# Attention of a graph network on one Trainium2 core: POOL's gathers wait, two at a time, for PE's sum of a tile

## The chip, the cores and the metric

The kernel runs on one core of one Trainium2 chip. The metric is the time on the device in microseconds (us) for one execution; lower is better. Engines are called PE (matmul), PEld (its weight load), DVE (vector), ACT (scalar), POOL (GpSimd) and SP (which issues DMAs).

## The reference

There are 6250 nodes of 128 features and 206250 edges, sorted by their target node `dst`. Two layers follow one another, each on `relu(layernorm(x))` and each with a residual. The change lies in the first:

```
h = (x @ W.T).reshape(N, 4, 32)
alpha = leaky_relu((h*att_src).sum(-1)[src] + (h*att_dst).sum(-1)[dst])
w = exp(alpha - segment_max(alpha, dst)[dst]);  w = w / segment_sum(w, dst)[dst]
out = segment_sum(h[src] * w[:, :, None], dst)
```

The second layer is an MLP on `[x[dst], x[src], edge_attr]` for each edge, summed over `src`'s partner in the same way; the change doesn't touch it.

## The kernel before, in words

The edges are cut into 1612 tiles of 128 edges, and the tiles into `NB` = 62 batches of `BT` = 26. The attention runs over the batches; a batch is a row of 26 turns, one for each tile, on PE, ACT and DVE, which are tied together by semaphores only. Each engine's order is written out by hand; the loops (`Fori`) hold two batches, `q` = 0 and 1.

In turn t of batch b:

- **DVE** makes the one-hot rows of tile t of batch b+2 (`hot`, L934), adds PE's sum of tile t-2 of batch b to the accumulator (`add_up`, L1041), and does one step of the softmax chain of batch b+1 (`chain`; at turn 4 the step "logits", which waits for all 26 gathers of batch b+1) or some products of messages (`product`, L1021, which ends in `msg_ready`).
- **PE** transposes the one-hot rows (`turn`, L1452), expands the node terms of tile t-1 of batch b+2 (`expand`, L1462), and sums the messages of tile t of batch b by a matmul with the one-hot rows (L1524), which raises `agg_ready`.
- **ACT** copies PE's transposed rows out (`turn_out`, L620) and widens one-hot rows to f32 (`widen`, L627).
- **POOL** does nothing in the attention but gather. `gather(i, q)` fetches for each tile of batch b = 2i+q the rows `h[src]` by one indirect DMA of 128 rows of 528 bytes into `G[:, q, t, :]` (L491). There are two slots `q`, so the gathers of batch b overwrite those of batch b-2 and run while batch b-2 is summed. They wait for the products of b-2 that read them: the first 13 for message pieces 0 and 1, the other 13 for pieces 2 and 3. So they come in two bursts of 13.

The order of PE within a turn matters below: `turn(b+2, t)`, then `expand(b+2, t-1)`, which waits for ACT's copy of tile t-1, and then the sum of tile t. ACT in turn waits for PE's transposes, and DVE's `add_up` for PE's sum; PE has two PSUM banks for each of the two.

At the end of the attention (L507) POOL waits for all sums, and does vector work for the nodes. In the target stretch of the second layer POOL scatters a finished tile by an indirect DMA (L541), in groups of three or four that wait for ACT's copies of them (L702). In the source stretch it issues one gather with addition at a time (L555), each behind a wait.

Of the kernel before, what the change touches and what calls it, by code (L numbers as in the profile page):

```python
# [25 lines left out]
BT = 26  # L26
# [39 lines left out]
def gnn(nc, x, src, dst, ea, W, asrc, adst, bias, W1, b1, W2, b2, out):  # L66
# [12 lines left out]
    with ctx:  # L79
# [4 lines left out]
        def sem(name):  # L84
            if name not in sems:
                sems[name] = ctx.enter_context(nc.semaphore(name))
            return sems[name]
# [355 lines left out]
        def _(pool):  # L443
# [39 lines left out]
            def gather(i, q, first=False):  # L483
                pool.wait_ge(sem("idx_ready"), 2 * i + q + 1)
                for h in range(2):

                    if not first:
                        pool.wait_ge(sem("msg_ready"), 4 * (2 * i + q - 2) + 2 * h + 2)
                    pool.nop(nofuse=True)
                    for t in range(h * (BT // 2), (h + 1) * (BT // 2)):  # L490
                        pool.indirect_dma_start(G[:, q, t, :], None, h_tab,  # L491
                                                bass.IndirectOffsetOnAxis(ap=idx[:, q, t:t + 1], axis=0)
                                                ).then_inc(sem(f"gath{q}"), 16)
            gather(0, 0, True)
            pool.wait_ge(sem("cols_used"), 2)
            gather(0, 1, True)
            pool.wait_ge(sem("hx_used"), NCH)
            M.memset(zlate, 0.0).then_inc(sem("zl_ready"), 1)
# [5 lines left out]
            with pool.Fori(1, NB // 2) as i:  # L504
                for q in range(2):
                    gather(i, q)
# [1241 lines left out]
```

## Time and profile before

| | us |
|---|---|
| median of 3 runs | 8049.95 |
| the runs | 8098.06, 8049.95, 8049.9 |
| the profiled execution, its own time | 8039.81 |
| its span, first to last instruction | 8038.0 |
| mean granted clock of TensorE in it | 0.808 |

The stages in the profiled span: preparation to about 200 us, attention to about 3770 us, node work to about 3900 us, targets to about 6650 us, sources to the end. "Slices" below are 40 equal parts of the span, so one is 201 us.

### The profile page before, as it was taken

To read this page: it belongs to the slowest core of one execution; us is meant where nothing else is said; L and a number is where in the kernel's file an instruction comes from. 1 tells how busy PE (TensorE), PEld (TensorE's weight loads), DVE (VectorE), ACT (ScalarE), POOL (GpSimd) and SP (SyncE) were. 2 spreads that over 40 slices of the span, in tenths; PEclk is the share of its full clock that TensorE was granted. 3 is DMA by queue.
4 is the path that set the end of the run, shared out by engine and by line. 5 is a ranking of instruction groups with operands and counts; after the bars stand their busy time and mean duration, and the time that the engine had idled before them with its cause. 6 is when DMAs were issued, how large, how long until landed. Compare 5 with 4: busy or idle time off the path is not lost.

```text
span 8038.0 us, 156599 instructions
## 1 busy us (share of the span) xinstructions
PE 5687.3 (71%) x34498; PEld 4372.6 (54%) x34499; DVE 4041.5 (50%) x14406; ACT 2887.4 (36%) x8241; POOL 3876.0 (48%) x3713
## 2 busy tenths in 40 slices
PE   4555555555555555555777878877877778999999
PEld 3444444444444444444555555555555556777777
DVE  5444444444444444446433434333333337888887
ACT  2333333333333333333222222222222226777776
POOL 4444344443444444443555555555555555555553
PEclk6666666667666666667889898898988889999999
DMA  3311111111111111113766666666656667999998
GB/s 86 110 31 30 29 31 31 30 31 29 31 31 30 30 30 31 31 31 111 210 188 194 194 196 196 197 191 189 192 168 202 188 190 189 213 213 213 215 212 197
DMA packets 860288, 993.30 MB, mean 124 GB/s; under 512 B 307992, under 2 KB 663224, under 8 KB 859774
## 3 DMA queue, kind: packets, MB, share of 16 engines
q1 hardware_dynamic: 662494, 608.23, 28.4%
q0 software_dynamic: 190592, 378.22, 17.6%
q10 hardware_dynamic: 6816, 3.38, 0.1%
q14 instruction: 348, 2.85, 0.1%
q8 instruction: 38, 0.62, 0.0%
HBM read 726.65 MB, written 262.76 MB: 123 GB/s over the span
## 4 chain that ended last, share of the span: by engine, by line
PE 55%; another core or an unknown queue 18%; issue 14%; DVE 8%; DVEq 3%; ACT 2%; DMA 1%; ACTq 0%; SPq 0%; POOLq 0%
PE bank L1524 12%; PE bank L1683 9%; PE bank L1618 8%; PE bank L1616 7%; PE bank L1673 5%; PE bank L1452 3%; PE bank L1462 2%; PE bank L1606 2%; DVEq L246 1%; DVE arena L1041 1%; PE bank L1571 1%; PE bank L1664 1%; DVE arena L1190 1%; ACT arena L620 1%
## 5 line engine op out<-in xcount | busy, mean ns | idle before, releaser
L491 POOL DMA_INDIRECT arena<-h_tab,arena x1612 | 1550.1, 962 | 2119.4 <-DVE arena L1021 1620.4
L541 POOL DMA_INDIRECT xr<-arena x1612 | 1581.5, 981 | 1233.9 <-ACT arena L702 753.9
L1524 PE MATMUL bank<-arena 128*128 128x136 f32 x6448 | 1527.6, 374 | 92.5 <-DVE arena L1041 9.5
L1041 DVE TENSOR_TENSOR arena<-arena,bank 128x272 f32 x1612 | 695.5, 431 | 1669.0 <-remote 1175.7
L620 ACT ACTIVATE arena<-bank 128x256 bf16<-128x256 bf16 x1612 | 617.5, 383 | 2413.1 <-remote 1190.1
L1618 PE MATMUL bank<-arena 128*128 128x256 f32 x3224 | 1107.3, 428 | 472.5 <-DVE arena L1251 383.6
L702 ACT ACTIVATE arena<-bank 128x256 f32<-128x256 f32 x1612 | 601.1, 384 | 2138.0 <-PE bank L1618 1276.8
L1462 PE MATMUL bank<-arena 128*128 x3224 | 427.8, 188 | 1273.5 <-ACT arena L620 641.4
L1524 PEld LDWEIGHTS bank<-arena 128*128 128x128 f32 x6448 | 1150.6, 247 | 178.3 <-issue 111.0
L1616 PE MATMUL bank<-arena 128*128 128x256 f32 x3224 | 1104.9, 427 | 11.6 <-DVE arena L1235 9.7
L1462 PEld LDWEIGHTS bank<-arena 128*128 128x128 bf16 x3224 | 325.3, 113 | 1378.3 <-issue 1343.1
L1618 PEld LDWEIGHTS bank<-arena 128*128 128x128 f32 x3224 | 650.2, 211 | 692.7 <-DVE arena L1251 482.4
L555 POOL DMA_INDIRECT arena<-p_tab,arena x428 | 667.8, 1560 | 662.0 <-DMA arena<-p_tab,arena 434.7
L1683 PE MATMUL bank<-arena 128*128 128x257 f32 x3424 | 897.4, 384 | 4.3 <-ACT arena L779 2.9
L1251 DVE COPY arena<-bank 128x128 f32<-128x128 f32 x806 | 233.2, 289 | 900.6 <-PE bank L1606 357.9
L627 ACT ACTIVATE arena<-arena 128x256 f32<-128x256 bf16 x1612 | 645.7, 408 | 87.1 <-issue 66.6
L1235 DVE TENSOR_SCALAR arena<-arena 128x128 f32<-128x128 bf16 x1612 | 471.6, 300 | 386.1 <-PE bank L1618 239.3
L1616 PEld LDWEIGHTS bank<-arena 128*128 128x128 f32 x3224 | 595.2, 217 | 113.4 <-issue 45.0
L1452 PE MATMUL bank<-arena 128*128 128x128 bf16 x3224 | 542.6, 260 | 123.4 <-DVE arena L934 112.5
L1683 PEld LDWEIGHTS bank<-arena 128*128 128x128 f32 x3424 | 584.9, 191 | 75.6 <-issue 6.5
L779 ACT ACTIVATE arena<-arena 128x512 f32<-128x512 f32 x856 | 535.5, 626 | 98.4 <-DVE arena L1346 77.9
L1673 PE MATMUL bank<-arena 128*128 x3852 | 566.7, 274 | 2.3 <-DVE arena L1346 1.7
(253 smaller groups left out, 6954.6 us busy)
## 6 DMA issues: line engine op xcount, KB each, us to landing
arena<-xr SPq DMA_DIRECT2D x428, 516.0 KB
arena<-q_tab SPq DMA_DIRECT2D x1612, 128.0 KB
arena<-in_edge_attr SPq DMA_DIRECT2D x61, 832.0 KB
arena<-rel_tab SPq DMA_DIRECT2D x124, 224.0 KB
arena<-h_tab,arena POOLq DMA_INDIRECT x1612
xr<-arena POOLq DMA_INDIRECT x1612
arena<-rel_tab SPq DMA_DIRECT2D x124, 192.0 KB
xr<-arena SPq DMA_DIRECT2D x26, 516.0 KB
```

What stands on the lines that cost most here:

```text
L491: pool.indirect_dma_start(G[:, q, t, :], None, h_tab, bass.IndirectOffsetOnAxis(ap=idx[:, q, t:t + 1], axis=0)).then_inc(sem(f"gath{q}"), 16)
L541: pool.indirect_dma_start(xr, bass.IndirectOffsetOnAxis(ap=pos[:, q, t:t + 1], axis=0), Rb[:, t, :], None).then_inc(sem(f"scat{m}"), 16)
L555: pool.indirect_dma_start(XR[:, s, k, RW:RW + HID], None, p_tab, bass.IndirectOffsetOnAxis(ap=sidx[:, s, k:k + 1], axis=0), compute_op=ALU ...
L620: A.activation(ohT[:, t % 2, :], PSB[t % 2][:].bitcast(BF16)[:, 0:2 * P], ACT.Copy).then_inc(sem("ohT_ready"), 1)
L1041: V.tensor_tensor(a, a, PSB[3 + t % 2][:, 0:2 * H * MW], ALU.add).then_inc(sem("acc_done"), 1)
L1452: last = pe.transpose(PSB[t % 2][:].bitcast(BF16)[:, k * P:(k + 1) * P], OHb[:, s, t, k * P:(k + 1) * P], identb)
L1462: last = pe.matmul(ab_ps[half][:, j, :, :].rearrange("p s c -> p (s c)"), ohT[:, t % 2, k * P:(k + 1) * P], flat(aT3[:, bass.ds(regs[t] + ...
L1524: last = pe.matmul(PSB[3 + t % 2][:, k * H * MW:(k + 1) * H * MW], OH[:, (t + 2 * q) % 4, k * P:(k + 1) * P], flat(msg[:, t, :, :]), start ...
L1616: pe.matmul(o, OHT[:, (t + 2 * q) % 4, :], Qw[:, t, :], start=True, stop=False)
L1618: pe.matmul(o, EAT[:, (t // 2 + q) % 2, :], w1z[:, t % 2, :], start=False, stop=True).then_inc(sem("main_done"), 1)
L1673: last = pe.matmul(PSB[2 + m % 2][:, j * HID:(j + 1) * HID], ohTp[:, m % 2, j, :], flat(Pt[:, bass.ds(reg, 1), part, :]), start=(part == 0 ...
L1683: last = pe.matmul(PSB[4 + m % 2][:, 0:XW], OHp[:, m, j, :], hid[:, m % 2, j, :], start=(j == 0), stop=(j == PR - 1))
```

## The change

Within each half, the gather of every odd tile first waits until PE has summed the tile of the same number in the batch whose slot it overwrites. The gather of the next (even) tile follows it at once. The first two batches, which overwrite nothing, are as before.

```
@@ gather(i, q, first=False)
                     pool.nop(nofuse=True)
                     for t in range(h * (BT // 2), (h + 1) * (BT // 2)):
+                        if not first and t % 2 == 1:
+                            pool.wait_ge(sem("agg_ready"), BT * (2 * i + q - 2) + t + 1)
+                            pool.nop(nofuse=True)
                         pool.indirect_dma_start(G[:, q, t, :], None, h_tab,
                                                 bass.IndirectOffsetOnAxis(ap=idx[:, q, t:t + 1], axis=0)
                                                 ).then_inc(sem(f"gath{q}"), 16)
```

## Rows read from the trace of the kernel before

**Rows 1.** The page: the granted clock in 40 slices, in tenths.
```profile
PEclk6666666667666666667889898898988889999999
```

**Rows 2.** Windows of attention, targets and sources: busy us (instructions) by engine.
```profile
400.00:3600.00 3200.00, 1793.45 (x12608) 1526.97 (x12608) 1487.92 (x5593) 1027.55 (x3203) 1338.02 (x1404) 0.68 0.13 30
4300.00:5900.00 1600.00, 1269.74 (x6293) 857.49 (x6291) 626.88 (x2243) 382.71 (x1104) 907.74 (x926) 0.90 0.66 193
6800.00:7800.00 1000.00, 984.33 (x6467) 776.98 (x6464) 813.08 (x2908) 738.13 (x1941) 504.00 (x323) 1.00 0.91 213
```

**Rows 3.** The timeline of POOL over two bursts of 13 gathers.
```profile
2008.45 0.95 POOL L491 DMA_INDIRECT arena<-h_tab,arena  x1 [15.56 <-DVE arena L1021]
2009.71 0.95 POOL L491 DMA_INDIRECT arena<-h_tab,arena  x1 [0.31 <-issue]
...
2023.53 0.95 POOL L491 DMA_INDIRECT arena<-h_tab,arena  x1 [0.30 <-issue]
2034.86 0.95 POOL L491 DMA_INDIRECT arena<-h_tab,arena  x1 [10.38 <-DVE arena L1021]
...
2049.98 0.95 POOL L491 DMA_INDIRECT arena<-h_tab,arena  x1 [0.30 <-issue]
```

**Rows 4.** Windows of one batch, DVE's L1041 alone (one per turn): us, busy (x).
```profile
2008.45:2026.80 18.35, 1.75 (x4) 0.55 0.21 49
2026.80:2034.86 8.06, 2.68 (x7) 0.75 0.00 0
2034.86:2053.20 18.34, 2.07 (x5) 0.67 0.22 48
2053.20:2065.48 12.28, 4.73 (x11) 0.80 0.00 1
```

**Rows 5.** The timeline of ACT inside the second of these bursts.
```profile
2042.75 0.38 ACT L620 ACTIVATE arena<-bank 128x256 bf16<-128x256 bf16 x1 [4.35 <-issue]
...
2051.32 0.39 ACT L620 ACTIVATE arena<-bank 128x256 bf16<-128x256 bf16 x1 [7.88 <-issue]
```

**Rows 6.** The timeline of PE at the same place.
```profile
2044.81 0.42 PE L1452 MATMUL bank<-arena 128*128 128x128 bf16 x2
2051.86 0.35 PE L1462 MATMUL bank<-arena 128*128 x2 [6.63 <-issue]
```

**Rows 7.** Windows: data movement after the first burst: us, busy of five engines, clock, DMA share.
```profile
2010.00:2024.50 14.50, 7.05 (x35) 5.90 (x35) 4.56 (x17) 2.80 (x10) 11.13 (x12) 0.51 0.25 57
2024.50:2026.20 1.70, 0.00 (x0) 0.00 (x0) 0.54 (x3) 0.28 (x1) 0.00 (x0) 0.50 0.19 40
2026.20:2027.40 1.20, 0.82 (x4) 0.70 (x5) 0.45 (x2) 1.20 (x5) 0.00 (x0) 0.50 0.00 0
```

**Rows 8.** The waits of 400 to 3600 us: engine and line, for whom, us, times, longest.
```profile
POOL arena L491 <- DVE arena L1021: 1457.5, 108, 16.5
...
DVE arena L1041 <- remote: 1076.8, 218, 10.6
ACT arena L620 <- remote: 1018.4, 142, 10.6
```

**Rows 9.** Line L491, 400 to 3600 us: shortest, median and longest duration in ns.
```profile
L491 POOL DMA_INDIRECT arena<-h_tab,arena x1404: 946/952/1002, 411.2 to 3585.6; - x176
```

**Rows 10.** Windows of the last two batches, L1524 alone (four matmuls per turn).
```profile
3720.00:3770.80 50.80, 37.70 (x208) 30.59 (x208) 0.90 0.11 33
```

**Rows 11.** The timeline of DVE from the last sum of batch 60 on.
```profile
3747.80 0.44 DVE L1041 TENSOR_TENSOR arena<-arena,bank 128x272 f32 x1 [0.34 <-PE bank L1524]
...
3750.66 0.44 DVE L1041 TENSOR_TENSOR arena<-arena,bank 128x272 f32 x1
...
3752.65 0.44 DVE L1041 TENSOR_TENSOR arena<-arena,bank 128x272 f32 x1 [0.38 <-PE bank L1524]
```

**Rows 12.** The waits of ACT and PE in the targets, 4300 to 5900 us.
```profile
ACT arena L702 <- issue: 278.8, 198, 4.7
...
ACT arena L702 <- remote: 237.2, 83, 8.2
...
PE bank L1618 <- DVE arena L1251: 218.1, 107, 6.5
PE bank L1618 <- issue: 49.6, 35, 6.0
```

**Rows 13.** Sources: ACT's longest group of waits (6800 to 7800 us), and one gather.
```profile
ACT arena L763 <- PE bank L1664: 125.0, 216, 1.2
...
7002.04 1.58 POOL L555 DMA_INDIRECT arena<-p_tab,arena  x1 [1.82 <-DMA arena<-p_tab,arena]
```

More of the change, by code:

```diff
@@ L490, in gather @@
                     for t in range(h * (BT // 2), (h + 1) * (BT // 2)):
+                        if not first and t % 2 == 1:
+                            pool.wait_ge(sem("agg_ready"), BT * (2 * i + q - 2) + t + 1)
+                            pool.nop(nofuse=True)
                         pool.indirect_dma_start(G[:, q, t, :], None, h_tab,
```

## The prediction, made before the changed kernel was run

> **What bounds the kernel now.** I began with the page's slices: the attention, about 45% of the span, has a granted clock of 0.6 to 0.7 where the last stages have 0.9 [rows 1]. In the windows by stage no engine is the bound there: in 3200 us PE is busy 1793, DVE 1488, ACT 1028 and POOL 1338 [rows 2]. 1404 gathers in these 3200 us are 54 batches, so a batch takes 3200 / 54 = 59.3 us. An engine with 33 us of work in 59 doesn't set that; something stops all of them.
>
> The timeline of POOL shows where to look. Its 26 gathers of a batch come in two bursts of 13, each gather 1.256 us behind the last (2009.71 - 2008.45), so a burst lasts 13 x 1.256 = 16.3 us, and POOL then waits 10 to 16 us for the next pieces of messages [rows 3, 8]. I cut one batch into four windows at these borders, the burst with the 2 us or so until its last data are in, and counted DVE's sums, one for each turn [rows 4]. Outside the bursts 7 + 11 = 18 turns take 8.06 + 12.28 = 20.3 us, 1.13 us each. Inside them 4 + 5 = 9 turns take 36.7 us, 4.1 us each. That is the finding on which all else rests: while gathers are issued back to back, the other engines hardly get on.
>
> How they stand still: PE ends the transposes of a tile at 2045.23 (2044.81 + 0.42) and ACT's copy of such rows starts at 2051.32, after 7.88 us of idleness that the profile puts down to nothing; PE then waits 6.63 us for that copy [rows 5, 6]. DVE has 218 such waits on "remote", 1077 us in all, and ACT 142, 1018 us; none of them has a late producer that the profile shows [rows 8]. The standstill ends with the burst: the last gather of the burst starts at 2049.98, ACT goes on 1.3 us later.
>
> **The price of a gather now.** In the four windows, bursts cost 36.7 us, less 9 turns at 1.13 (10.2 us), less about 3 us for the border between two batches (register loads and the factor), which falls into the first burst; I size it by the last batches, where the sum of the last tile and of the next batch's first are 3750.66 - 3747.80 = 2.9 us apart [rows 4, 11]. That leaves 23.5 us, or 0.90 us for each of 26 gathers; I use 0.93, the mean of this and of the same count with the border at 1.5 us (0.96). A batch with gathers that cost nothing would take 59.3 - 26 x 0.93 = 35.1 us. Two rows bear this out: the last two batches gather nothing and take 50.8 / 2 = 25.4 us, without the work on tiles of the batch two ahead [rows 10]; and 26 turns at 1.13 with the border are 29.4 + 3 = 32.4 us.
>
> **The change part by part.**
>
> *Added waits.* 13 for each of 60 batches (2 to 61), each a register sum, a wait and a nop on POOL's queue. Behind such a wait stand only the rest of the gathers; POOL has no other work in the attention, and its work for the nodes waits for all sums anyway. POOL needs 26 x 1.256 = 32.7 us for a batch's gathers. The waits have no row of their own; between gathers stand 0.30 us today [rows 3]. The cost on POOL lies between 0 (inside these 0.30) and 13 x 0.3 = 3.9 us, so its floor is 32.7 to 36.6 us per batch, below or near the 35.1 of the others. I count nothing on the path, as the forecast batch is far above both.
>
> *Moved gathers.* Now gather 1 goes when tile 1 of batch b-2 is summed, then 2 and 3, and so on; the last, tile 25, goes when PE has summed tile 25 of b-2. Who waits for that is DVE's step "logits" at turn 4 of batch b-1, behind `add_up` of tile 2. In the last batches tile 25's sum and tile 2's of the next batch are 3752.65 - 3747.80 = 4.85 us apart at DVE [rows 11]. One gather needs some 0.95 us of issue, and the traffic of a burst is over at most 2.7 us after its last gather began (2026.20 - 2023.53; no traffic after) [rows 3, 7]. So 2.7 of 4.85 us, hidden, with room for one or two gathers of arrears. POOL collects arrears when turns are faster than 1.256 us, as they are outside bursts (1.13): 26 turns x 0.13 = 3.3 us at most, from which the slow border of batches subtracts 3. Counted at nothing; with the cover gone (arrears of three gathers, 3.8 us) DVE waits 2.7 + 3.8 - 4.85 = 1.7 us per batch, 100 us in all.
>
> *What the spacing removes.* This is the term that decides. With the two-gather steps, a pair takes 2.5 us and two turns take at least 2.3, so POOL pauses only as long as the engines are held up; but that is also when it counts: as soon as DVE, ACT and PE stand still, POOL stops within two gathers instead of running on for up to 13. The trace of before has no pairs in the attention, so the price per gather after has bounds. Upper: 0.93, today's. Lower: 0, from the sources, where single gathers come 3.1 us apart (1000 / 323), traffic is at 0.91, and the longest wait in ACT's largest group is 1.2 us; nothing is held up [rows 2, 13]. Below nothing is excluded: no gather can speed the engines over having none. Between them lie the targets: 926 scatters in groups of 3 and 4 that sometimes run together. If all of PE's waits at L1618 were theirs, that is (218.1 + 49.6) / 926 = 0.29 us each; if I take ACT's waits without a producer, (278.8 + 237.2) / 926 = 0.56 us each, again the most [rows 2, 12]. These are nearest to what the change makes: short groups, at times joined. I take the middle, 0.43 us. The attention has tighter buffers (two banks, not four), which speaks for more; pairs are shorter than those groups, which speaks for less.
>
> *The sum.* A batch then takes 35.1 + 26 x 0.43 = 46.3 us, 13.0 less than 59.3. Over 60 batches that is 780 us: 8040 - 780 = 7260 for the profiled execution, whose 8039.8 lies 10 us below the median of the runs; against the median, 7270. In general the time is 8050 - 1560 x (0.93 - p) for a price p. A denser attention should also raise the granted clock there above 0.68, as the windows outside bursts (0.75 and 0.80) show against 0.55 in the first burst [rows 2, 4]; this is contained in the pace of 1.13 and not counted again.
>
> *A rule against it.* All of L491's gathers take 946 to 1002 ns, so DVE doesn't hold up POOL's descriptors at all [rows 9], and data movement is at a quarter of its capacity in a burst [rows 7]. The Trainium skill (SBUF — State Buffer, in the consequences drawn from the port table) states "DMA never contends with a compute engine", and knows only the reverse, a DVE instruction that starves POOL's descriptor generation. By that rule the bursts would hold nothing up, p would stay at 0.93 and the time at 8050; by the rows the engines stand still in just these windows. The trace has the decision, and I can't name the mechanism from it.
>
> **The rivals.**
>
> *1. The burst isn't the cause (nothing gained, 8050).* The bursts start on DVE's products, so they always lie at the same turns (about 0 to 3 and 11 to 15); the standstill could belong to these turns, to the chain's steps or the loading of instructions. For it: the fixed place. Against it: waits without a producer are there in the targets too, beside scatters, and not in the sources with their spaced gathers [rows 12, 13]. The rule above gives the same time. 0.09.
>
> *2. A fixed price per gather or per group (slower).* If each group of gathers costs a fixed standstill of some microseconds, 13 pairs replace two bursts. The point of decision is 24.2 / 13 = 1.9 us per pair. ACT's shortest standstills in the second burst are over 4 us [rows 5]; a pair costs at most what it and its landing last, 2.5 + 1.5 = 4 us, but of this about half is covered by buffers. At 2.1 us per pair a batch takes 35.1 + 27.3 + 1.7 for late gathers = 64.1 us, 4.8 more: 8050 + 60 x 4.8 = 8340. 0.10.
>
> *3. Pairs cost nothing, POOL becomes the bound.* Then a batch takes POOL's floor of 36 to 38 us: at 37, 60 x 22.3 = 1340 us less, 6710. For it: the sources. Against: POOL would then issue without a pause, which is the burst again. 0.12, with prices below 0.25 (up to 6990).
>
> *4. The pairs join.* When turns run at 1.13 us POOL has no pause, gathers join to groups of 6 to 10, and the price is 0.70 to 0.88: 7690 to 7970. 0.11.
>
> **How the numbers follow.** The forecast (price 0.25 to 0.70, 6990 to 7690) has 0.58; its likeliest is 7270. The range should leave out no more than 2 in 10: it goes from 6900 (part of rival 3) to 7950 (nearly all of rival 4), and leaves out rivals 1 and 2 and the lower end of 3. A measurement of this kernel can tell about 1% from no change. Faster by over 1%: 0.58 + 0.12 + 0.11 = 0.81; within 1%: rival 1, 0.09; slower: rival 2, 0.10.
>
> **What would show it.** After the change POOL's L491 should stand in pairs with pauses of a microsecond or so, released by PE at L1524, and its waits on DVE at L1021 should be gone. A batch should last 46 us, the attention end near 2990 instead of 3770 us, and later stages be unchanged. DVE's waits on "remote" at L1041 should fall from 1077 to some 450 us, and the longest from 10.6 to about 4 us. The clock in the attention should be above 0.70. Rival 3 shows as POOL without idleness; rival 4 as long rows of gathers behind idleness of 0.30 us; rival 1 as standstills at turns 3 and 14 beside a pausing POOL; rival 2 as 13 of them in a batch. A wait of DVE at L953 for a gather would show late gathers. What would make me wrong most likely is the price of a pair, which no row of this kernel measures in a loop as tight as the attention's.

## The result

| | before | after |
|---|---|---|
| median, us | 8054.2 (4 runs, 8049.9 to 8098.1) | 7419.5 (4 runs, 7395.8 to 7434.7) |
| ratio, 95% interval | | 0.920 (0.916 to 0.923) |
| span of the profiled execution | 8038.0 | 7415.3 |
| mean granted clock | 0.808 | 0.828 |

The change saves 635 us. The forecast was 7270 in a range of 6900 to 7950. The experiments below are compared apart from this table, each with the kernel before on its own chip.

The changed kernel's lines are three further down from L494 on (L491 is L494, L1524 is L1527, L1041 is L1044). The page's clock in 40 slices of what is now a shorter span, as in [rows 1]:

```profile
PEclk6777777766767776779988888898888889999999
```

Windows of three stretches, to be laid beside [rows 2] (busy us and instructions of PE, PEld, DVE, ACT, POOL; clock; DMA share; GB/s):

```profile
400.00:2900.00 2500.00, 1807.33 (x11880) 1530.26 (x11881) 1424.75 (x5273) 959.68 (x3019) 1305.21 (x1332) 0.71 0.17 37
3700.00:5300.00 1600.00, 1277.29 (x6281) 863.10 (x6281) 625.39 (x2231) 379.26 (x1098) 904.86 (x921) 0.89 0.66 192
6200.00:7200.00 1000.00, 984.58 (x6471) 777.75 (x6469) 814.14 (x2910) 738.94 (x1941) 505.46 (x324) 1.00 0.92 213
```

1332 gathers in 2500 us are 51.2 batches, 48.8 us each instead of 59.3; 10.5 us less in 60 batches are 630 us, the whole gain. Targets and sources move as much per us as before (921 scatters in 1600 us beside 926, 324 gathers in 1000 beside 323). So nothing was given back later.

POOL's timeline over some gathers, to be read beside [rows 3]:

```profile
2032.58 0.95 POOL L494 DMA_INDIRECT arena<-h_tab,arena  x1 [6.92 <-PE bank L1527]
2033.84 0.95 POOL L494 DMA_INDIRECT arena<-h_tab,arena  x1 [0.30 <-issue]
2035.38 0.95 POOL L494 DMA_INDIRECT arena<-h_tab,arena  x1 [0.60 <-issue]
...
2039.34 0.99 POOL L494 DMA_INDIRECT arena<-h_tab,arena  x1 [1.75 <-PE bank L1527]
...
2049.28 0.95 POOL L494 DMA_INDIRECT arena<-h_tab,arena  x1 [4.19 <-issue]
2050.53 0.95 POOL L494 DMA_INDIRECT arena<-h_tab,arena  x1 [0.30 <-issue]
2051.79 0.95 POOL L494 DMA_INDIRECT arena<-h_tab,arena  x1 [0.30 <-issue]
2053.05 0.95 POOL L494 DMA_INDIRECT arena<-h_tab,arena  x1 [0.30 <-issue]
2054.31 0.95 POOL L494 DMA_INDIRECT arena<-h_tab,arena  x1 [0.30 <-issue]
2055.57 0.95 POOL L494 DMA_INDIRECT arena<-h_tab,arena  x1 [0.30 <-issue]
```

The wait is PE's now, as meant. But the gathers often don't come in pairs: six stand together at 2049.28. POOL had fallen behind (ahead of them it stood idle for 4.19 us that no late producer explains), all its waits were fulfilled, and it ran on until it caught up. Counted over 600 to 2000 us, with a gap of 0.5 us or more as the border of a group, 745 gathers stand in 280 groups: 195 pairs, 75 fours, 9 sixes and one alone, 2.7 on average. The other engines pay for the joined ones, as ACT's timeline shows:

```profile
2057.18 0.38 ACT L623 ACTIVATE arena<-bank 128x256 bf16<-128x256 bf16 x1 [5.86 <-remote]
```

The waits of 400 to 2900 us, beside [rows 8]:

```profile
ACT arena L623 <- PE bank L1455: 915.9, 755, 4.6
POOL arena L494 <- PE bank L1527: 728.4, 367, 7.0
DVE arena L1044 <- PE bank L1527: 591.4, 596, 3.9
...
ACT arena L623 <- remote: 412.2, 148, 5.9
...
DVE arena L1044 <- remote: 214.4, 97, 5.2
```

DVE's waits on "remote" fall from 1077 us in 54 batches to 214 in 51, ACT's from 1018 to 412, and the longest from over 10 to under 6 us. This reads better than it is, for part of the late waits only has another label now: the rows that name PE as the releaser were these before.

```profile
ACT arena L620 <- PE bank L1452: 707.8, 812, 4.0
DVE arena L1041 <- PE bank L1524: 327.9, 442, 4.7
```

Both labels together, DVE waited for PE's sums (1076.8 + 327.9) / 54 = 26.0 us per batch and now waits (214.4 + 591.4) / 51.2 = 15.7. These 10.3 us are nearly the 10.5 by which a batch got shorter. No group of DVE's waits names a gather: none came late.

### The profile page after: what moved, and what is told of

It reads as the page before. It is cut to its first block, busy times and chain, and to the rows that moved or that the text cites. A ratio compares the mean times of both kernels' runs of the same rounds, so it can differ in the third digit from the quotient of the medians.

```text
span 7415.3 us, 158159 instructions
## 1 busy us (share of the span) xinstructions
PE 5830.3 (79%) x34498; PEld 4483.9 (60%) x34499; DVE 4072.9 (55%) x14406; ACT 2876.8 (39%) x8241; POOL 3921.0 (53%) x3713
## 4 chain that ended last, share of the span: by engine, by line
PE 66%; another core or an unknown queue 12%; issue 10%; DVE 6%; DVEq 3%; ACT 2%; DMA 1%; ACTq 0%; POOL 0%; SPq 0%; POOLq 0%
PE bank L1527 16%; PE bank L1686 10%; PE bank L1621 9%; PE bank L1619 8%; PE bank L1676 6%; PE bank L1455 4%; PE bank L1465 4%; PE bank L1609 2%; DVEq L246 2%; ACT arena L623 1%; PE bank L1574 1%; PE bank L1667 1%; DVE arena L1193 1%; DVE arena L1238 1%
## 5 line engine op out<-in xcount | busy, mean ns | idle before, releaser
L494 POOL DMA_INDIRECT arena<-h_tab,arena x1612 | 1592.0, 988 | 1474.2 <-PE bank L1527 857.6
L1527 PE MATMUL bank<-arena 128*128 128x136 f32 x6448 | 1625.0, 392 | 77.6 <-DVE arena L1044 6.2
L1527 PEld LDWEIGHTS bank<-arena 128*128 128x128 f32 x6448 | 1227.4, 263 | 149.2 <-issue 108.6
L1044 DVE TENSOR_TENSOR arena<-arena,bank 128x272 f32 x1612 | 699.9, 434 | 1006.3 <-PE bank L1527 689.8
L1621 PEld LDWEIGHTS bank<-arena 128*128 128x128 f32 x3224 | 655.6, 212 | 707.7 <-DVE arena L1254 450.2
L1465 PE MATMUL bank<-arena 128*128 x3224 | 442.3, 193 | 526.5 <-ACT arena L623 406.5
L1465 PEld LDWEIGHTS bank<-arena 128*128 128x128 bf16 x3224 | 350.3, 121 | 645.8 <-issue 606.8
L1455 PE MATMUL bank<-arena 128*128 128x128 bf16 x3224 | 563.5, 268 | 134.4 <-DVE arena L937 132.4
L1619 PEld LDWEIGHTS bank<-arena 128*128 128x128 f32 x3224 | 597.9, 218 | 111.2 <-issue 40.1
L1686 PEld LDWEIGHTS bank<-arena 128*128 128x128 f32 x3424 | 585.5, 191 | 74.6 <-issue 5.2
L937 DVE TENSOR_SCALAR arena<-arena 128x256 bf16<-128x256 bf16 x1612 | 456.3, 287 | 220.5 <-issue 211.2
```

The costliest lines, as they stand in the source:

```text
L494: pool.indirect_dma_start(G[:, q, t, :], None, h_tab, bass.IndirectOffsetOnAxis(ap=idx[:, q, t:t + 1], axis=0)).then_inc(sem(f"gath{q}"), 16)
L1044: V.tensor_tensor(a, a, PSB[3 + t % 2][:, 0:2 * H * MW], ALU.add).then_inc(sem("acc_done"), 1)
L1455: last = pe.transpose(PSB[t % 2][:].bitcast(BF16)[:, k * P:(k + 1) * P], OHb[:, s, t, k * P:(k + 1) * P], identb)
L1465: last = pe.matmul(ab_ps[half][:, j, :, :].rearrange("p s c -> p (s c)"), ohT[:, t % 2, k * P:(k + 1) * P], flat(aT3[:, bass.ds(regs[t] + ...
L1527: last = pe.matmul(PSB[3 + t % 2][:, k * H * MW:(k + 1) * H * MW], OH[:, (t + 2 * q) % 4, k * P:(k + 1) * P], flat(msg[:, t, :, :]), start ...
L1619: pe.matmul(o, OHT[:, (t + 2 * q) % 4, :], Qw[:, t, :], start=True, stop=False)
```

## The experiments

Each ratio is against the kernel before on the same chip. Experiments 1 to 8 ran on three chips, on which the kernel before took 7935 to 7945 us and not 8054 as in the first comparison (its chip isn't on record). A forecast in microseconds that was made from 8054 is to be read some 110 us lower there. "Us per batch" is worked out from a window of 1400 us in the attention (600 to 2000 us), in which DVE's sums (one per tile, 26 per batch) are counted: 1400 x 26 / count. Here are those rows for the kernel before, for the changed one, and for seven of the experiments, each named ahead of its row. Before (59.4 us):

```profile
600.00:2000.00 1400.00, 264.50 (x613) 0.68 0.13 31
```

After (48.9 us):

```profile
600.00:2000.00 1400.00, 323.61 (x745) 0.70 0.17 37
```

**1. No gathers.** All gathers after the first two batches are gone, and the wait for them; messages are made from old rows.

(The total that later stages wait for on the gathers' semaphore, `GSUM`, is lowered to match.)

```diff
-            with pool.Fori(1, NB // 2) as i:
-                for q in range(2):
-                    gather(i, q)
...
-                    dve.wait_ge(sem(f"gath{q}"), 16 * BT * (i + 1))
+                    if isinstance(i, int) and i == 0:
+                        dve.wait_ge(sem(f"gath{q}"), 16 * BT)
```

> The kernel before without any gather after the first two batches; DVE doesn't wait for them, and the messages are made from old rows. It gives the floor, and beside the loads issued by SP the price of the traffic itself. Theory 'POOL's issue': a batch as with SP's loads (33.4 us) or up to 1 us less, so 6420 to 6490 us where that one had 6483. Rival 'transfers cost too': over 2 us per batch less, under 6370 us.

6441.2 us, ratio 0.812 (0.811 to 0.813). The row:

```profile
600.00:2000.00 1400.00, 469.99 (x1096) 0.89 0.00 1
```

33.2 us per batch. With the two rows above, a gather in a burst costs (59.4 - 33.2) / 26 = 1.01 us, one after the change (48.9 - 33.2) / 26 = 0.60 us. But those two rows are from the first comparison, where the kernel before takes 110 us longer than on the chip of this experiment. On one and the same chip the price in a burst is (7935.6 - 6441.2) / 1560 = 0.96 us, and the row of experiment 4, which keeps the bursts, gives 57.9 us per batch and 0.95. The saving of the change is 634.6 / 1560 = 0.41 us per gather. So the price is 0.95 to 1.01 us in bursts and 0.55 to 0.60 after the change: the first comparison has some 1.5 us more per batch, and no run tells whether they belong to its floor or to its gathers. The granted clock is 0.89 in this window: an attention that isn't held up runs mostly at the upper of TensorE's two levels.

**2. As many rows, issued by SP.** Plain loads of 128 consecutive rows of 528 bytes, in the same bursts behind the same waits; messages are made from other rows. POOL's loop of gathers is taken out as in experiment 1, and DVE waits for these loads instead.

```diff
+            with sp.Fori(1, NB // 2) as i:
+                for q in range(2):
+                    sp.wait_ge(sem("idx_ready"), 2 * i + q + 1)
+                    for h in range(2):
+                        sp.wait_ge(sem("msg_ready"), 4 * (2 * i + q - 2) + 2 * h + 2)
+                        sp.nop(nofuse=True)
+                        for t in range(h * (BT // 2), (h + 1) * (BT // 2)):
+                            sp.dma_start(G[:, q, t, :], h_tab[t * P:(t + 1) * P, :]).then_inc(...)
```

> The gathers after the first two batches are replaced by plain loads of as many rows of the same size (128 rows of 528 bytes, consecutive ones, so the messages are made from other rows), issued by SP in the same bursts of 13 behind the same waits. POOL issues nothing in the loop. Theory 'POOL's issue': no standstills, near the kernel without gathers, about 6600 us. Rival 'transfers' (the engines are held up by what arrives, whoever issues it): 8050 us, or at least over 7500.

6483.1 us, ratio 0.818 (0.816 to 0.820), 33.3 us per batch. "Transfers" falls: as many bytes arrive, in bursts, and nobody is held up. (They are read from consecutive rows, which the gathers are not.)

**3. The same loads, issued by POOL.** The kernel before, but with `pool.dma_start(G[:, q, t, :], h_tab[t * P:(t + 1) * P, :])` in place of each indirect gather after the first two batches.

> As the kernel with SP's plain loads (same rows, same bursts of 13, messages made from other rows), but POOL issues them. Only the issuing engine differs from that one, only the indirect addresses from the kernel before. Theory 'POOL's issue': the standstills are back, 7700 to 8050 us, or somewhat less if a plain load takes POOL less time. Rival 'scattered rows' (reading 128 places of HBM is what holds the others up): as SP's loads, about 6480 us.

6436.3 us, ratio 0.812 (0.810 to 0.813). My theory, "POOL's issue" as such, missed by over 1200 us. The timeline shows full bursts of 13, and the window the pace of the kernel without gathers (33.3 us):

```profile
1515.28 6.87 POOL L492 DMA_DIRECT2D arena<-h_tab  x13 [12.51 <-DVE arena L1024]
```

```profile
600.00:2000.00 1400.00, 469.00 (x1093) 0.90 0.22 54
```

Thirteen plain loads take POOL 6.87 us, 0.53 each, so they come faster than the gathers (1.256 us apart) and still hold up nobody. What does is the indirect form, or the scattered addresses that only it can reach.

**4. Half the bytes.** The kernel before with 264 bytes for each row instead of 528 (`h_tab.rearrange("n (a f) -> (n a) f", a=2)` into `G[:, q, t, 0:GW // 2]`); the other half of the messages is made from old data. By the code, index i names half row i of the table here, so the addresses are scattered too but lie in half of it.

> The kernel before, its bursts of 13 unchanged, but each gather after the first two batches fetches 128 rows of 264 bytes instead of 528 (half of each row; the rest of the message rows is old data). Same number of descriptors, half the bytes. Theory 'issue' (what POOL does to make and hand over descriptors holds up the others): unchanged, 8050 us, and the same standstills. Rival 'traffic' (bytes that move): the price halves, 8054 - 1560 x 0.47 = 7320 us.

7937.4 us, ratio 0.9994 (0.9984 to 1.0004). Unchanged within 0.1%: the number of indirect DMAs or of their descriptors counts, not their bytes. The row of DVE's sums, 57.9 us per batch:

```profile
600.00:2000.00 1400.00, 272.57 (x629) 0.70 0.10 16
```

**5. The second burst, three turns later.** One wait more ahead of gathers 13 to 25: `agg_ready` for tile 14.

> The kernel before with one wait more: the second burst of 13 also waits for PE's sum of tile 14, so it starts about three turns later. Theory 'gathers': the second standstill moves from turns 13 to 15 to turns 16 to 18, time within 2% of before, 7950 to 8200 us. Rival 'fixed turns': it stays at turns 13 to 15.

7999.4 us in one run, beside 7935.5. The sums of DVE before that burst and in it, and the burst's first gather:

```profile
2027.90:2044.40 16.50, 6.42 (x15) 0.90 0.02 4
2044.40:2060.80 16.40, 0.90 (x3) 0.62 0.22 50
```

```profile
2042.42 0.95 POOL L493 DMA_INDIRECT arena<-h_tab,arena  x1 [16.51 <-PE bank L1526]
```

And DVE's timeline in the kernel before, where this burst starts at 2034.86 [rows 3]:

```profile
2036.44 0.44 DVE L1041 TENSOR_TENSOR arena<-arena,bank 128x272 f32 x1 [0.16 <-issue]
...
2042.26 0.44 DVE L1041 TENSOR_TENSOR arena<-arena,bank 128x272 f32 x1 [4.74 <-remote]
...
2049.42 0.44 DVE L1041 TENSOR_TENSOR arena<-arena,bank 128x272 f32 x1 [6.35 <-remote]
```

There the sums of tiles 12 and 13 are late, 5.8 and 7.2 us after the one before. With the burst moved, 15 sums run through tile 16 in 16.5 us, 1.1 us each, and then the window of the burst has two (a third only by its tail): the standstill is at tiles 17 to 19. It moved with the burst. The rival "fixed turns" falls.

**6. Other group sizes.** `if not first and t >= 1:` (one at a time) and `if not first and t % 4 == 1:` (four) in place of the change's `t % 2 == 1`.

> Every gather but tile 0's waits for PE's sum of the same tile two batches back, so gathers come one at a time. Theory 'run length' (the price of a gather grows with how many stand back to back: 0.93 us in 13, 0.53 in pairs): 0.3 to 0.4 us, 7070 to 7230 us. Rival 'price per wait or per group': 26 groups cost more than 13, slower than pairs, 7600 us or more. If POOL's queue has caught up anyway, as pairs often join, the same as pairs, 7420.

> The same wait at every fourth gather (tiles 1, 5, 9, ...). Theory 'run length': between pairs (7420) and bursts (8054), about 7600 to 7750 us. Rival 'any brake is enough' (what counts is that POOL stops soon after the others do): as pairs, 7400 to 7500. Rival 'price per group': faster than pairs.

One at a time: 7307.5 us, ratio 0.9195 (0.9175 to 0.9215); four: 7513.2, ratio 0.946 (0.944 to 0.948). The rows of DVE's sums, one at a time and then four:

```profile
600.00:2000.00 1400.00, 333.25 (x767) 0.72 0.17 38
```

```profile
600.00:2000.00 1400.00, 311.41 (x718) 0.66 0.16 36
```

They give 47.5 and 50.7 us per batch, so with the floor of 33.2 the price per gather is 0.55 us (one) and 0.67 (four), beside 0.95 in bursts of 13 on these chips (row of experiment 4) and 0.55 to 0.60 for pairs. Some two thirds of the gain come already with a wait at every fourth gather (432 us of 635); from four to one it is 3 us per batch. "Price per group" falls, since 25 waits cost no more than 13. Of the theories' numbers, "run length" missed for one at a time, which it wanted 190 us or more below pairs; the case named beside it, "the same as pairs", came true. For four it fits once the 110 us are taken off, and "any brake is enough" doesn't.

Two and one have the same ratio although one waits twice as often, because the wait doesn't pace POOL when it is behind: of POOL's idle times ahead of a gather in this window, 445 with one at a time are the bare 0.3 us or so. Counted in groups as above, one at a time makes 280 groups of 2.7 gathers, just as pairs do, and every fourth makes 185 groups of 3.9. What the queue did, not what was asked of it, goes with the price.

```profile
POOL arena L494 <- PE bank L1527: 416.7, 268, 7.2
POOL arena L494 <- issue: 151.3, 445, 0.7
```

**7. A fixed pause instead of PE's sum.** The kernel before with, ahead of each odd gather, a write of 640 words per partition that POOL waits for.

(`scr` is new, 640 words per partition.)

```diff
+                        if not first and t % 2 == 1:
+                            M.memset(scr, 0.0).then_inc(sem("pads"), 1)
+                            pool.wait_ge(sem("pads"), 13 * (2 * i + q - 2) + t // 2 + 6)
+                            pool.nop(nofuse=True)
```

> The kernel before, with no wait on PE, but POOL writes 640 words per partition to an unused place before every odd gather and waits for that, about 0.8 us, so pairs stand apart by a fixed pause. Theory 'pauses' (the gap alone lets the others on): about as with the change, 7350 to 7550 us. Rival 'feedback' (what counts is that POOL stops when the others stand still): POOL runs on during a standstill, 7700 us or more.

7327.5 us, ratio 0.924 (0.922 to 0.927), 48.3 us per batch. As with the change, but by another way (23 us below the expected range, inside it once the 110 us are taken off). POOL's timeline, and the waits of 600 to 2000 us:

```profile
2002.24 0.65 POOL L493 MEMSET arena<- 128x640 f32 x1
2003.65 0.98 POOL L496 DMA_INDIRECT arena<-h_tab,arena  x1 [0.75 <-POOL arena L493]
2004.94 0.95 POOL L496 DMA_INDIRECT arena<-h_tab,arena  x1 [0.31 <-issue]
```

```profile
DVE arena L958 <- DMA arena<-h_tab,arena: 269.1, 29, 14.2
...
DVE arena L1046 <- remote: 6.4, 7, 1.4
```

DVE's waits on "remote" are gone (6.4 us, where the kernel before has 480 in the same window). What is left is POOL itself: pairs stand 3.6 us apart, 13 of them are 47 us, and DVE waits for late gathers (269 us in 29 times). Pauses alone free the engines; no feedback from PE is needed.

**8. A shorter pause, and a rarer one.** The same with 128 words; and the long one before every fourth gather only.

> As the kernel with a fixed pause before every odd gather, with 128 words written instead of 640: the pause shrinks by some 0.45 us, POOL needs 41 us for a batch instead of 47. There the standstills were gone and DVE waited 9 us per batch for late gathers. Theory 'a short pause suffices': 42 to 44 us per batch, 7000 to 7130 us. Rival 'the pause has to be a full microsecond': standstills return, 7300 us or more.

> The long pause (640 words) before every fourth gather: POOL needs 32.7 + 7 x 1.1 = 40.4 us. Theory 'what counts is idleness of POOL in all': as the small pause in pairs, 7000 to 7130 us. Rival 'what counts is how many stand together': groups of four hold the others up as they did with the wait on PE, 7400 us or more.

The short pause: 7016.4 us, ratio 0.883 (0.882 to 0.885), the fastest here on these chips that gathers the right rows. Its row gives 42.4 us per batch, and its pairs are 3.2 us apart:

```profile
600.00:2000.00 1400.00, 371.57 (x858) 0.80 0.19 42
```

```profile
1500.23 0.22 POOL L493 MEMSET arena<- 128x128 f32 x1
1501.21 0.96 POOL L496 DMA_INDIRECT arena<-h_tab,arena  x1 [0.75 <-POOL arena L493]
1502.47 0.95 POOL L496 DMA_INDIRECT arena<-h_tab,arena  x1 [0.30 <-issue]
```

13 x 3.2 is 41.6 us: POOL is nearly all of it, and DVE's "remote" is 1.0 us in the window, though it still waits 140 us there for late gathers, 4 us per batch. The long pause at every fourth: 7344.3 us, ratio 0.926 (0.924 to 0.928), 48.1 us per batch, although POOL needs only about 40. So it isn't POOL's idleness in all that counts but how many gathers stand together: a gap of 0.97 us after every second frees the others nearly, one of 1.4 us after every fourth doesn't.

**9. Scattered or consecutive rows; a bare instruction as a pause.** The kernel before with indices 0 to 127 for every tile; and the pause without its wait, 48 words written before each odd gather.

```diff
-                V.tensor_scalar(idx[:, s, :], srcE[:, bass.ds(b * BT, BT)], 0.0, None, ALU.max)...
+                V.tensor_scalar(idx[:, s, :], pcol[:, 0:1].to_broadcast([P, BT]), 0.0, None, ALU.max)...
```

```diff
+                        if not first and t % 2 == 1:
+                            M.memset(scr[:, t // 2, :], 0.0).then_inc(sem("pads"), 1)
```

> The kernel before with its indirect gathers and bursts of 13 unchanged, but every list of indices is 0 to 127, so each gather reads the same 128 consecutive rows (the messages are made from other rows). Issuer, instruction and count are as before; only the addresses in HBM aren't scattered. Theory 'the indirect form' (what POOL does for an indirect DMA holds the others up): unchanged, 7850 to 8000 us beside 7940. Rival 'scattered rows': no standstills, about 6440 us as with plain loads.

> As the small pause in pairs, but POOL only writes 48 words before each odd gather and doesn't wait for it: the pause shrinks from about 1.0 to some 0.4 to 0.5 us in place of 0.30. Theory 'any other instruction between pairs suffices': POOL's floor of 35 to 36 us is what is left, 6550 to 6700 us. Rival 'it is the length of the pause': standstills come back, 7400 us or more.

These two ran on another chip, and there the kernel before took 5764.6 us (19 runs, 5759.4 to 5772.1), not 7940. Consecutive rows: 5762.6 us, ratio 0.9995 (0.9986 to 1.0005). The bare instruction: 5774.1 us, 1.0018 (1.0008 to 1.0027). There the indirect gathers hold up nobody, so there is nothing to cure and neither question is answered. All runs on this chip belong to this one comparison, so whether the chip itself or something else about it at that time makes the difference isn't shown. The kernel before has no trace from it; the traces are of the two kernels named here. The consecutive rows' windows in attention and targets, and POOL's idle times in the attention:

```profile
600.00:2000.00 1400.00, 468.10 (x1091) 0.90 0.22 54
```

```profile
2400.00:3400.00 1000.00, 947.10 (x5365) 676.93 (x5363) 541.63 (x1911) 326.76 (x941) 763.20 (x778) 1.00 0.93 262
```

```profile
POOL arena L491 <- issue: 321.2, 1054, 0.3
```

The attention runs at 33.4 us per batch, the floor of experiment 1, while POOL issues gathers without any gap but 0.30 us (1054 times). The targets go faster as well: 778 scatters per 1000 us, where the chip of the first profile has 926 in 1600, and move 262 GB/s instead of 193 [rows 2].

## Why the prediction was right, and what in it was wrong

- **What bounds it.** "While gathers are issued back to back, the other engines hardly get on" was right, and the experiments show it: without gathers 33.2 us per batch, with the burst moved the standstill moves.
- **What exactly is late.** "DVE, ACT and PE stand still" is too coarse. I paired each wait with the instruction it waits for, in the trace of before (400 to 3600 us). DVE has 299 waits of over 1 us for PE's sum; in 237 of them it goes on more than 1 us after the end that the profile gives for the sum, 4.6 us in the median of all 299. PE has 174 waits of over 1 us for ACT's copy and 27 for DVE's one-hot rows, and every one ends within 0.16 us of the copy's or the rows' end. So only what PE hands on arrives late, and PE then stands still for want of those whom it kept waiting. Without gathers (experiment 1), with POOL's plain loads (3) and with the consecutive rows of experiment 9, no such wait for a sum ends over 0.3 us after it. As the ends of matmuls are modelled in a profile, it can't be told whether PE's work ends late or the news of it.
- **The base.** I took 35.1 us for a batch with free gathers and 0.93 us for a gather; measured were 33.2 and 0.95 to 1.01. Much of the miss is a count. The five sums of the third window in [rows 4] hold the tail of one that began at 2034.77, in the window before:

```profile
2034.77 0.42 DVE L1041 TENSOR_TENSOR arena<-arena,bank 128x272 f32 x1
```

With 8 turns in the bursts instead of 9 the same sum gives 0.95 and 1.01 us, mean 0.98, and 33.8 us for the batch.
- **Added waits.** Nothing on the path: right. 12 more for one at a time cost nothing either.
- **Late gathers.** Counted at nothing: right; DVE has no wait for a gather. In experiment 7, with POOL at 47 us per batch, this cover was gone, at 9.3 us per batch.
- **The deciding term was mis-sized.** I predicted 0.43 us per gather after the change, from the targets' short groups; it is 0.60 with the floor of 33.2, or 0.55 if the extra time of the first comparison lies in its floor. The likely cause is rival 4 in part: the gathers join whenever POOL is behind, and nearly half of them (47% in 600 to 2000 us) stand in groups of four or six. With 0.60, that is 0.17 x 26 = 4.4 us per batch more than forecast; the floor is 1.9 us lower than I took it; the 2.5 us that remain are, times 60, the 150 us between 7270 and 7420. The middle of 0.29 and 0.56 had no better ground than lying between two bounds, and the upper one was nearly the price; that the time came out so close owes something to the base, whose error ran the other way.
- **The rule.** The trace spoke against "DMA never contends with a compute engine" (the Trainium skill, SBUF — State Buffer, the practical consequences under "Who interferes with whom"). The runs give the rule its due and its bound: plain loads of as many rows hold up nobody, from SP or from POOL (33.3 us per batch), and half the bytes change nothing. So it isn't the number of bytes. But indirect DMAs issued back to back did hold up the others, by about 1 us each, in every comparison but the last. Whether that is contention with the moving of scattered data, or with the making of the descriptors, no run shows.
- **Rival 1** fell by experiment 5, **rival 2** by the change itself: two groups per batch became about ten, and the batch got shorter. **Rival 3**, POOL as the bound, isn't reached by the change, but by the short pause.
- **The clock.** I expected over 0.70 in the attention; it is 0.71, and 0.89 without standstills. The prices per gather hold what the lower clock costs too; no run parts the two.

**What stays open.** Why an indirect DMA holds up the others, and why on one chip it doesn't. The form of the instruction and the scattered addresses weren't told apart, since the run meant for it fell on the chip without the effect. One more way, that gathers hold up the loading of instructions, has little for it: plain loads did no harm, and in the trace of before (600 to 2000 us) the packets that load instructions take 0.44 us in the median beside gathers' packets (86) and 0.46 without (45). The change itself wasn't run on that chip; its attention ran at the floor there already, so no gain is to be expected, and for the bare pause the loss is bounded, at 0.3%.

## What to carry to other kernels

When engines stand still for microseconds with no late producer in the trace, lay their gaps beside the timeline of every queue, the off-path ones too: here they matched POOL's bursts of indirect DMAs, which moved little (31 GB/s). Then ask whose work it is that arrives late; here it was PE's alone. Break such bursts by a pause after every second one, no longer than it takes to free the others. Here 0.97 us did; a shorter one wasn't tried where it matters. A wait on the consumer works too, but stops working once the issuer is behind. Compare prices only within one chip. And time both kernels on more than one chip before such a cure is kept: on one of them there was nothing to cure.

## What wasn't expected of the hardware

- The same program took 7935 to 7945 us on three chips and 5765 us on a fourth, and 8054 us in the first comparison, each within 1%.
- In a burst of indirect gathers DVE goes on up to 10.6 us after the end that the profile gives for PE's sum, while PE, where it waits for ACT or DVE, goes on within 0.16 us.
- Thirteen plain loads of 128 rows on POOL's queue take 6.87 us and disturb nobody; thirteen indirect ones of the same size take 16.3 us and cost the others 12 to 13 us.
- A write of 128 words with a wait for it, 0.97 us in all between pairs, took away nearly all of DVE's waits without a producer (1.0 us left in 1400).
